# Keys of a large attention turned from their natural layout, two batches ahead, with the queries made in the other batch of each pair

## The chip, the cores and the metric

One NeuronCore of a Trainium2 chip runs the whole program. The metric is the device time of one execution in microseconds (us). The five engines of the core each work through their own list of instructions in order and wait for one another by semaphores: TensorE (PE, matrix products), VectorE (DVE), ScalarE (ACT), GpSimd (POOL) and SyncE (SP, which issues the DMA transfers).

## The reference

A small "perceiver": x is 32 batches of 64 rows of 256; a context is 32 batches of 1601 rows of 64. Two layers follow one another: attention to the context, self-attention and an MLP in the first; attention to the whole context, self-attention and a mixture of 16 experts in the second. The change touches only the second layer's attention to the context:

```python
q_hk = (hidden_q @ Wq.T).reshape(Bv, Sv, H, K)          # 64 rows, 16 heads of 128
q_big = apply_rope(einsum('bshk,hkq->bshq', q_hk, w_kc_q), sin_q, cos_q)
kv_r = apply_rope(kv_c, sin_k, cos_k)                   # 1601 keys of 64
q_r = einsum('bshq,hqr->bhsr', q_big, W_qr)
k_r = einsum('bld,hdr->bhlr', kv_r, W_kr)
attn = softmax(einsum('bhsr,bhlr->bhsl', q_r, k_r), axis=-1)
ctx_c = einsum('bhsl,bld->bhsd', attn, kv_r)            # then w_kc_kv and Wo
```

`apply_rope(x)` is `x * cos + rotate_half(x) * sin`, and rotate_half moves the upper half of the row in front with a changed sign. hidden_q is the layer-normalised x.

## The kernel before, in words

The matrices are combined once, so that a query of 64 numbers meets the rotated keys directly. The attention (`context_attention`) then runs over B = 32 batches of the context. Two batches share one block of 128 rows of x, so t counts NT = 16 pairs; e is 0 in the even batch 2t and 1 in the odd batch 2t+1. In each batch the 16 heads times 64 rows make 1024 columns of queries (two halves p of 512), and the 1601 keys are cut into NKT = 13 key tiles kt of 128 (the last has 65). In the text a "step" is one kt of `batch`. `batches` writes out batch 0 and the last three, and repeats a loop body of one odd and one even batch 14 times.

What one step of batch n does, by engine:

- PE: `scores` of the next key tile for p = 0 and 1 (two products into one bank, with k1 and k2), and `values` of this one. Each `scores` waits until ACT has taken the exponentials of the tile before it from the same bank. Between them, by third of a step, stand the pieces of other work: `max_scores` (16 pieces, scores of the next batch for its maxima, two banks mx in turn), `queries` (ten in five steps: `big`, then two later `effective`), `turn_keys`, `denominators` (step 0), `out` (OUT_AT = 4, even batch), `max_rows` (ROWS_AT = 10 and 11).
- ACT: `exps` of both halves, and the copies out of PSUM.
- DVE: `add` (the sum of the exponentials for p = 1), `reduce_max` (one for each of the 16 pieces; two banks, so a piece waits for the reduction two before it), `negate_max`, `invert` and `scale_heads` (steps 2 and 3), `rotate` and `split` (queries), `sum_keys` and `keep_kl` (keys), `normalise` and `update_x`.
- POOL: `add` for p = 0 and the two products of the keys' rotation.
- SP: `fetch` of the next context, twice (as it is and with its halves changed over).

Keys come from memory transposed (64 x 1608). They are rotated in four chunks of 402 columns (POOL lines 627 and 628, DVE line 977). ACT writes the rounded keys to k1 and to k2 (line 863), DVE the remainder to the lower half of k1 (line 982): k1 holds [kh; kl], k2 holds kh and a row of ones that adds minus the maximum. Thus the scores are exact to more than the rounded format. PE turns the sum kr in two parts at steps 6 and 7 to get the natural layout for `values` (kv). `max_scores` of the next batch reads k1 of the next batch, which is why k1 and k2 are kept at steps 0 and 1 of the batch before. The queries of pair t+1 are made in the odd batch, steps 0 to 4 (lines 703, 717 on PE, 1004 on DVE, 890, 891 on ACT), and its pieces for the maximum start at step 5; in the even batch they start at step 3. They end before ROWS_AT in both. x is normalised at step 10 of the even batch, and `turn_x` stands ahead of step 0 of the odd one. prob has three buffers in a ring and one for the last tile.

Of the kernel before, what the change touches and what calls it, by code (L numbers as in the profile page):

```python
# [481 lines left out]
def context_attention(nc, sb, pb, sem, a, x_all, const, wbig, mw, wvo):  # L482
# [12 lines left out]
    kcos = sb("cx_kcos", [DCX, SKP])  # L495
    ksin = sb("cx_ksin", [DCX, SKP])
    ctx = sb("cx_ctx", [DCX, SKP])
    ctxr = sb("cx_ctxr", [DCX, SKP])
    kr = sb("cx_kr", [DCX, SKP])
# [107 lines left out]
    with nc.Block() as block:  # L607

        @block.sync
        def _(sp):  # L610
            def fetch(n):
                sp.dma_start(ctx[:, :], a["cx_ctxT"][bass.ds(n, 1), :, :]).then_inc(s_ctx, 16)
                sp.dma_start(ctxr[:, :], a["cx_ctxrT"][bass.ds(n, 1), :, :]).then_inc(s_ctx, 16)

            fetch(0)
            with sp.Fori(1, B) as n:

                sp.wait_ge(s_kr, n * NKC)
                fetch(n)

        @block.gpsimd
        def _(pool):
            def rotate(n, c):
                cols = slice(c * KC, (c + 1) * KC)
                if c == 0:
                    pool.wait_ge(s_ctx, 32 * n + 32)
                pool.tensor_tensor(ctx[:, cols], ctx[:, cols], kcos[:, cols], ALU.mult)  # L627
                pool.tensor_tensor(ctxr[:, cols], ctxr[:, cols], ksin[:, cols], ALU.mult).then_inc(s_rope, 1)
# [1239 lines left out]
```

## Time and profile before

| | |
|---|---|
| time, median of 3 runs | 3492.59 us (3492.21 to 3497.96) |
| profiled execution: its time / its span | 3504.15 us / 3501.6 us |
| PE busy | 2942.5 us, 84% |
| DVE busy | 2084.2 us, 60% |
| ACT busy | 1277.2 us, 36% |
| POOL busy | 900.8 us, 26% |
| batch 6 (even), end to end | 1121.24 to 1170.48 us |
| batch 7 (odd), end to end | 1170.48 to 1240.73 us |

The span is what lies between the first and the last instruction of the profiled execution; the execution's own time is 2.6 us above it. Busy shares are means over stages with different limits. The attention that changes takes the stretch from about 690 to 2640 us. A batch ends where ACT copies the finished values out (line 928).

### The profile page before, as it was taken

How to read it: one execution, taken by the hardware profiler on the slowest of the kernel's cores; microseconds unless marked ns; L12 is line 12 of the kernel's file. 1: busy time of each engine (PE TensorE's matmuls, PEld its weight loads, DVE VectorE, ACT ScalarE, POOL GpSimd, SP SyncE). 2: the span in 40 equal slices, each digit the busy share in tenths (PEclk: the TensorE clock that was granted, in tenths of full speed). 3: DMA queues.
4: the chain of work that ended last, by engine and by line, in shares of the span. 5: the costliest groups of instructions: out<-in, count | busy, mean ns of one | idle time of the engine just before them, and what ended most of it. 6: DMA issues, size and time to landing. Idle time of an engine off the chain costs nothing. (4 is left out here: it accounts for less than half of the span.)

```text
span 3501.6 us, 51568 instructions
## 1 busy us (share of the span) xinstructions
PE 2942.5 (84%) x17592; PEld 1773.8 (51%) x17592; DVE 2084.2 (60%) x3249; ACT 1277.2 (36%) x2482; POOL 900.8 (26%) x784
## 2 busy tenths in 40 slices
PE   6767734579988988898898889888996889999999
PEld 3544412445544544454455445444543457777776
DVE  3445567357686777677776877686775643333332
ACT  3433312123344343434334433444343333333332
POOL 0001000134354444344434544453440000000000
PEclk9888856679999999999999999999999899999999
DMA  1000030000000000000000000000003000000000
GB/s 39 0 17 0 0 117 0 22 19 10 19 9 19 9 19 9 19 9 19 9 11 17 19 9 9 19 9 19 10 0 145 0 0 0 0 0 0 0 0 25
DMA packets 15045, 57.83 MB, mean 17 GB/s; under 512 B 2512, under 2 KB 7248, under 8 KB 13584
## 3 DMA queue, kind: packets, MB, share of 16 engines
q1 hardware_dynamic: 13392, 53.57, 5.5%
q10 hardware_dynamic: 1600, 3.56, 0.3%
q8 instruction: 32, 0.52, 0.1%
q14 instruction: 21, 0.17, 0.0%
HBM read 55.03 MB, written 2.10 MB: 16 GB/s over the span
## 5 line engine op out<-in xcount | busy, mean ns | idle before, releaser
L917 ACT ACTIVATE cx_prob<-cx_st 128x512 f32<-128x512 f32 (+1 forms) x832 | 477.4, 596 | 742.8 <-PE cx_st L774 680.7
L645 POOL TENSOR_TENSOR cx_acc<-cx_acc,cx_prob 128x512 f32<-128x512 f32 (+1 forms) x352 | 493.8, 1403 | 751.5 <-ACT cx_prob L917 747.4
L1023 DVE TENSOR_REDUCE cx_mhalf<-cx_mx 128x1 f32<-128x804 f32 x512 | 491.2, 983 | 86.5 <-PE cx_mx L747 83.7
L785 PE MATMUL cx_av<-cx_prob,cx_kv 128*64 128x512 f32 (+1 forms) x1664 | 462.2, 635 | 0.0
L773 PE MATMUL cx_st<-cx_q,cx_k 128*128 128x512 f32 (+1 forms) x832 | 372.5, 448 | 84.5 <-ACT cx_prob L917 60.5
L1506 PE MATMUL moe_gu<-moe_wgu,moe_xnT 128*128 128x352 f32 x1280 | 399.0, 463 | 0.0
L1044 DVE TENSOR_TENSOR cx_acc<-cx_acc,cx_prob 128x512 f32<-128x512 f32 (+1 forms) x352 | 371.3, 1055 | 21.7 <-ACT cx_prob L917 19.9
L747 PE MATMUL cx_mx<-cx_k,cx_q 128*128 128x402 f32 x1024 | 309.3, 388 | 53.2 <-DVE cx_mhalf L1023 47.3
L1641 DVE SCALAR_TENSOR_TENSOR moe_hid<-moe_silu,moe_coef,moe_gu 128x176 f32<-128x176 f32 x320 | 127.1, 397 | 351.6 <-ACT moe_silu L1569 349.4
L774 PE MATMUL cx_st<-cx_q,cx_k 128*128 128x512 f32 (+1 forms) x832 | 332.8, 400 | 0.0
L747 PEld LDWEIGHTS cx_mx<-cx_k,cx_q 128*128 128x128 f32 x1024 | 173.4, 195 | 264.0 <-DVE cx_mhalf L1023 216.8
L1506 PEld LDWEIGHTS moe_gu<-moe_wgu,moe_xnT 128*128 128x128 f32 x1280 | 242.2, 191 | 124.9 <-issue 7.5
L773 PEld LDWEIGHTS cx_st<-cx_q,cx_k 128*128 128x128 f32 (+1 forms) x832 | 154.5, 186 | 267.2 <-ACT cx_prob L917 157.9
L1004 DVE TENSOR_TENSOR cx_turn<-cx_mx,cx_tab 128x384 f32<-128x384 f32 x256 | 130.9, 553 | 264.5 <-PE cx_mx L703 264.5
L1569 ACT ACTIVATE moe_silu<-moe_gu 128x176 f32<-128x176 f32 x320 | 101.8, 318 | 372.0 <-PE moe_gu L1506 372.0
L1529 PE MATMUL moe_acc<-moe_wd,moe_hidT 128*128 128x256 f32 (+1 forms) x896 | 216.1, 382 | 0.0
L703 PE MATMUL cx_mx<-cx_xnT,cx_wbig 128*128 128x128 f32 x1536 | 205.6, 284 | 2.3 <-ACT cx_xnT L879 0.5
L703 PEld LDWEIGHTS cx_mx<-cx_xnT,cx_wbig 128*128 128x128 f32 x1536 | 184.2, 193 | 26.9 <-issue 16.4
L717 PE MATMUL cx_mx<-cx_turn,cx_mw 128*64 128x128 f32 (+1 forms) x2048 | 197.0, 296 | 0.0
L1529 PEld LDWEIGHTS moe_acc<-moe_wd,moe_hidT 128*128 128x128 f32 (+1 forms) x896 | 160.2, 190 | 21.9 <-issue 5.3
L1471 POOL TENSOR_TENSOR moe_rstd<-moe_mv,minus_half 128x1 f32<-128x1 f32 x16 | 8.8, 549 | 614.8 <-DVE moe_mv L1606 614.8
L627 POOL TENSOR_TENSOR cx_ctx<-cx_ctx,cx_kcos 64x402 f32<-64x402 f32 x128 | 160.5, 1254 | 7.3 <-DMA cx_ctxr<-in_cx_ctxrT 7.3
(214 smaller groups left out, 3945.0 us busy)
## 6 DMA issues: line engine op xcount, KB each, us to landing
cx_ctx<-in_cx_ctxT SPq DMA_DIRECT2D x32, 402.0 KB, 4.3
cx_ctxr<-in_cx_ctxrT SPq DMA_DIRECT2D x32, 402.0 KB, 5.5
moe_wgu<-in_moe_wgu SPq DMA_DIRECT2D x5, 1408.0 KB, 15.3
moe_wd<-in_moe_wd SPq DMA_DIRECT2D x4, 896.0 KB, 25.0
x_all<-in_x SPq DMA_DIRECT2D x1, 2048.0 KB, 5.3
cx_wq<-in_cx_wq SPq DMA_DIRECT2D x1, 2048.0 KB, 12.0
cx_woT<-in_cx_woT SPq DMA_DIRECT2D x1, 2048.0 KB, 29.5
out_x<-x_all SPq DMA_DIRECT2D x1, 2048.0 KB, 7.5
```

Source lines behind the costliest of these rows:

```text
L645: pool.tensor_tensor(acc[0][rows, :], sofar, prob[slot(kt)][rows, 0, :], ALU.add)\
L703: last = pe.matmul(mx[j % 2][:, 0, tile * P:(tile + 1) * P], wbig[:, c, j, tile * P:(tile + 1) * P], xnT[:, c, :], start=(c == 0), stop=(c ...
L717: last = pe.matmul(mx[j // 4][DCX * e:DCX * e + DCX, 1, at:at + P], mw[rows, j, cs, tile, :], turn[j % 2][rows, cs, tile, :, :], start=(cs ...
L747: last = pe.matmul(mx[b][:, h, 0:KQ], q, k1[e][:, lo:lo + KQ], start=True, stop=True)
L773: pe.matmul(st[p][0:nk(kt), :], k1[e][:, keys], q1[e][:, p, :, :], start=True, stop=False)
L774: pe.matmul(st[p][0:nk(kt), :], k2[e][:, keys], q2[e][:, p, :, :], start=False, stop=True)\
L785: last = pe.matmul(av[DCX * p:DCX * p + DCX, :], kv[e][0:nk(kt), kt, :], prob[slot(kt)][0:nk(kt), p, :], start=(kt == 0), stop=(kt == NKT ...
L917: act.activation(prob[slot(kt)][rows, p, :], st[p][rows, :], ACT.Exp).then_inc(s_exp, 1)
L1023: dve.tensor_reduce(mhalf[:, i // 2, i % 2:i % 2 + 1], mx[i % 2][:, :, 0:KQ], AX.XY, ALU.max)\
L1044: dve.tensor_tensor(acc[1][rows, :], sofar, prob[slot(kt)][rows, 1, :], ALU.add)\
L1506: last = pe.matmul(gu[i][:, 0:2 * FE], xnT[g][:, c, :], wgu[:, e, c, :], start=(c == 0), stop=(c == DC - 1))
L1529: last = pe.matmul(acc[:, 0:D], hidT[q % 2][0:n, k % 4, :], wd[0:n, k, :], start=(k == 0), stop=(k == NFC - 1))
```

## The change

All of it is in the attention to the whole context and in how its inputs are laid out.

- The context, its turned copy and the cos and sin tables are laid out in the natural way, as tiles of 128 keys: [128, 13, 64]. The rotation of a whole batch of keys is two POOL products (step 3) and one DVE addition (step 4) of 128 x 832 elements.
- ACT copies the rounded keys to khl[:, :, 0, :] (step 4) and DVE subtracts them into khl[:, :, 1, :] (step 5). PE transposes 13 tiles of 128 x 128 in four rounds at steps 6 to 9, ACT copies each round from PSUM to a new buffer kp (steps 7 to 10). kp holds what k1 held. `max_scores` reads kp.
- All that is done for batch n + 2 in batch n. SP issues two transfers from kp to k1 and to the upper half of k2 when the batch that used k1 and k2 is over; `scores` reads k1 and k2 as before, and now waits for the transfers.
- kv is a plain ACT copy of kr (step 2). The four copies that filled k1, k2 and kv from kr and PSUM in each batch are gone.
- The queries of pair t+1 are made in the even batch, steps 7 to 11; x is normalised there at step 5 and turned at the end of step 6. ACT's `keep_queries` and DVE's `split` stand at steps 0 and 1, and 1 and 2, of the odd batch. The even batch's 16 pieces lie in steps 1 to 6, the odd batch's in steps 3 to 9.

```diff
+    SUM_AT = 4
+    NORM_AT = 5
     TURN_AT = 6
+    QUERIES_AT = 7
     ROWS_AT = NKT - 3
-    SUM_AT = (8, 9, 11, 12)
     def pieces(e, kt, third):
-        start, end = 3 * (5 if e else 3), 3 * ROWS_AT
+        start, end = (9, 3 * ROWS_AT) if e else (4, 3 * QUERIES_AT)
...
+            def move(n, e):
+                sp.wait_ge(s_kp, KROUNDS * (n + 1))
+                if not isinstance(n, int) or n >= 2:
+                    sp.wait_ge(s_st, (n - 1) * 2 * NKT)
+                sp.dma_start(k1[e][:, :].bitcast(F32), kp[e][:, 0:SKP].bitcast(F32)).then_inc(s_kd[e], 16)
+                sp.dma_start(k2[e][0:DCX, :].bitcast(F32), kp[e][0:DCX, 0:SKP].bitcast(F32)).then_inc(s_kd[e], 16)
...
+            def rotate(n):                                                      # POOL, step 3
+                pool.wait_ge(s_ctx, 32 * n + 32)
+                pool.tensor_tensor(ctx[:, :, :], ctx[:, :, :], kcos[:, :, :], ALU.mult)
+                pool.tensor_tensor(ctxr[:, :, :], ctxr[:, :, :], ksin[:, :, :], ALU.mult).then_inc(s_rope, 1)
...
+            def turn_keys(n, r):
+                if r == 0:
+                    pe.wait_ge(s_kl, n + 1)
+                else:
+                    pe.wait_ge(s_kp, KROUNDS * n + r)
+                for kt in range(4 * r, min(4 * r + 4, NKT)):
+                    last = pe.transpose(misc[:, kt % 4 * P:(kt % 4 + 1) * P], khl[:, kt, :, :], ident[:, :])
                 last.then_inc(s_kt, 1)
...
-                    last = pe.matmul(mx[b][:, h, 0:KQ], q, k1[e][:, lo:lo + KQ], start=True, stop=True)
+                    last = pe.matmul(mx[b][:, h, 0:KQ], q, kp[e][:, lo:lo + KQ], start=True, stop=True)
...
             def batch(n, t, e, more, next):                                     # PE
                 for kt in range(NKT):
-                    if kt == 0 and more and e == 1:
-                        turn_x(t + 1)
                     for third in range(3):
...
-                        if more and e == 1 and third < 2 and kt <= CP // 2:
-                            queries(t + 1, 2 * kt + third)
+                        if more and e == 0 and third < 2 and 0 <= kt - QUERIES_AT <= CP // 2:
+                            queries(t + 1, 2 * (kt - QUERIES_AT) + third)
                         if next:
                             for i in pieces(e, kt, third):
                                 max_scores(t + e, n + 1, 1 - e, i)
+                    if kt == QUERIES_AT - 1 and more and e == 0:
+                        turn_x(t + 1)
...
-                    if kt in (TURN_AT, TURN_AT + 1) and next:
+                    if 0 <= kt - TURN_AT < KROUNDS and more:
...
-                        turn_keys(n + 1, kt - TURN_AT)
+                        turn_keys(n + 2, kt - TURN_AT)
...
             def batch(n, t, e, more, next):                                     # ACT
-                    if kt == 0 and more and e == 1:
-                        keep_x(t + 1)
                     if kt == 0 and e == 0:
                         odd_queries(t)
-                    if kt == 0 and next:
-                        keep_keys(n + 1, 1 - e, k1, s_k1)
-                    if kt == 1 and next:
-                        keep_keys(n + 1, 1 - e, k2, s_k2)
-                    if kt in (3, 4) and more and e == 1:
-                        keep_queries(t + 1, kt - 3)
-                    if kt in (TURN_AT + 1, TURN_AT + 2) and next:
-                        keep_kv(n + 1, 1 - e, kt - TURN_AT - 1)
+                    if kt in (0, 1) and more and e == 1:
+                        keep_queries(t + 1, kt)
+                    if kt == 2 and next:
+                        keep_kv(n + 1, 1 - e)
+                    if kt == SUM_AT and more:
+                        keep_kh(n + 2)
+                    if kt == QUERIES_AT and more and e == 0:
+                        keep_x(t + 1)
+                    if 0 <= kt - TURN_AT - 1 < KROUNDS and more:
+                        keep_turned(n + 2, t + 1, e, kt - TURN_AT - 1)
...
             def batch(n, t, e, more, next):                                     # DVE
-                        if third < 2 and more and e == 1 and kt < CP // 2:
-                            rotate(t + 1, 2 * kt + third)
+                        if third < 2 and more and e == 0 and 0 <= kt - QUERIES_AT < CP // 2:
+                            rotate(t + 1, 2 * (kt - QUERIES_AT) + third)
...
-                    if kt == 1 and next:
-                        keep_kl(n + 1, 1 - e)
+                    if kt in (1, 2) and more and e == 1:
+                        split(t + 1, kt - 1)
...
-                    if kt in (3, 4) and more and e == 1:
-                        split(t + 1, kt - 3)
+                    if kt == SUM_AT and more:
+                        sum_keys(n + 2)
+                    if kt == SUM_AT + 1 and more:
+                        keep_kl(n + 2)
...
-                    if more and kt in SUM_AT:
-                        sum_keys(n + 2, SUM_AT.index(kt))
-                    if more and e == 0 and kt == ROWS_AT:
-                        normalise(t + 1, base + (2 if next else 0))
+                    if kt == NORM_AT and more and e == 0:
+                        normalise(t + 1, base)
```

## Rows read from the trace of the kernel before

**Rows 1.** The page: the chain that ended last, share of the span by engine.

```profile
PE 18%; issue 0%; DVE 0%; POOL 0%; ACT 0%; POOLq 0%
```

**Rows 2.** Windows, batches 6 and 7: length, busy of PE, PEld, DVE, ACT, POOL, clock, DMA.

```profile
1121.24:1170.48 49.24, 42.10 (x188) 21.88 (x189) 40.79 (x46) 22.31 (x36) 27.40 (x21) 1.00 0.04 8
1170.48:1240.73 70.25, 64.03 (x398) 36.20 (x399) 46.31 (x60) 25.35 (x47) 24.61 (x20) 0.98 0.06 13
```

**Rows 3.** PE's timeline, batch 31, the last: two steps without other work (start, us, instruction).

```profile
2606.03 0.50 PE L773 MATMUL cx_st<-cx_q,cx_k 128*128 128x512 f32 x1
...
2608.16 0.50 PE L773 MATMUL cx_st<-cx_q,cx_k 128*128 128x512 f32 x1
```

**Rows 4.** PE's timeline in even batch 6: its waits, in brackets with their releaser.

```profile
1125.93 0.50 PE L773 MATMUL cx_st<-cx_q,cx_k 128*128 128x512 f32 x1 [1.76 <-ACT cx_prob L917]
...
1140.08 3.72 PE L802 MATMUL cx_misc<-cx_wvo,cx_heads 128*128 128x256 f32 x16 [1.43 <-DVE cx_heads L1055]
...
1164.28 0.22 PE L760 MATMUL cx_misc<-cx_identb,cx_nmh 128*1 128x128 bf16 x1 [1.35 <-DVE cx_nml L1031]
...
1168.25 0.47 PE L773 MATMUL cx_st<-cx_q,cx_k 128*128 128x512 f32 x1 [0.76 <-ACT cx_q L921]
```

**Rows 5.** PE's timeline in odd batch 5, from turn_x to the first piece.

```profile
1050.28 0.44 PE L693 MATMUL cx_mx<-ident,cx_xn 128*128 128x128 f32 x2
...
1055.56 1.03 PE L795 MATMUL cx_misc<-cx_acc,cx_ones 128*64 128x512 f32 x4
...
1085.17 1.08 PE L785 MATMUL cx_av<-cx_prob,cx_kv 128*64 128x512 f32 x4
1088.23 0.50 PE L773 MATMUL cx_st<-cx_q,cx_k 128*128 128x512 f32 x1 [1.98 <-ACT cx_prob L917]
```

**Rows 6.** Groups of instructions by line and shape, both batches: count, busy, mean ns, idle before.

```profile
L1023 DVE TENSOR_REDUCE cx_mhalf<-cx_mx 128x1 f32<-128x804 f32 x32 | 30.7, 982 | 5.5 <-PE cx_mx L747 5.3
...
L747 PE MATMUL cx_mx<-cx_k,cx_q 128*128 128x402 f32 x64 | 19.0, 381 | 3.2 <-DVE cx_mhalf L1023 3.0
...
L627 POOL TENSOR_TENSOR cx_ctx<-cx_ctx,cx_kcos 64x402 f32<-64x402 f32 x8 | 10.1, 1262 | 0.0
...
L1050 DVE RECIPROCAL cx_rden<-cx_misc 128x256 f32<-128x256 f32 x4 | 7.0, 1746 | 0.0
...
L863 ACT CAST cx_k<-cx_kr 64x1608 fp32r<-64x1608 f32 x4 | 6.1, 1529 | 0.0
...
L982 DVE TENSOR_TENSOR cx_k<-cx_kr,cx_k 64x1608 fp32r<-64x1608 f32 x2 | 3.7, 1827 | 0.1
...
L890 ACT CAST cx_q<-cx_mx 64x256 fp32r<-64x256 f32 x8 | 2.9, 368 | 8.8 <-PE cx_mx L717 8.7
```

**Rows 7.** DVE's timeline in even batch 6: the odd queries, out's shadow, the normalisation.

```profile
1123.85 1.22 DVE L1018 TENSOR_TENSOR cx_q<-cx_qs,cx_q 64x1024 fp32r<-64x1024 f32 x1 [5.63 <-ACT cx_q L899]
...
1144.66 1.00 DVE L1023 TENSOR_REDUCE cx_mhalf<-cx_mx 128x1 f32<-128x804 f32 x1 [2.23 <-PE cx_mx L747]
...
1164.77 0.42 DVE L988 BATCH_NORM_STATS2 cx_stats<-x_all 128x6 f32 x1
...
1166.26 1.34 DVE L996 TENSOR_SCALAR cx_xn<-x_all,cx_mv,cx_rstd 128x256 f32 x1 [0.66 <-POOL cx_rstd L632]
```

**Rows 8.** Lines 1044 (add) and 977 (sum_keys), 1000 to 2600 us: min/median/max ns.

```profile
L1044 DVE TENSOR_TENSOR cx_acc<-cx_acc,cx_prob x297: 671/823/1873, 1009.6 to 2597.2; 128x512 f32<-128x512 f32 x135, 65x512 f32<-65x512 f32 x14
...
L977 DVE TENSOR_TENSOR cx_kr<-cx_ctx,cx_ctxr x104: 555/561/1855, 1038.9 to 2551.8; 64x402 f32<-64x402 f32 x104
```

**Rows 9.** Windows of 1 us in odd batch 7, PE: busy, then clock, DMA.

```profile
1209.00:1210.00 1.00, 1.00 (x7) 0.94 0.00 0
...
1211.00:1212.00 1.00, 1.00 (x4) 0.50 0.00 0
...
1213.00:1214.00 1.00, 1.00 (x5) 0.86 0.00 0
```

**Rows 10.** The page's DMA issues: count, KB each, median us to landing.

```profile
cx_ctxr<-in_cx_ctxrT SPq DMA_DIRECT2D x32, 402.0 KB, 5.5
```

More of the change, by code:

```diff
@@ L494, in context_attention @@
     tab = sb("cx_tab", [P, 2, 3, S])
[L495 to L499, printed above, removed]
+    kcos = sb("cx_kcos", [P, NKT, DCX])
+    ksin = sb("cx_ksin", [P, NKT, DCX])
+    ctx = sb("cx_ctx", [P, NKT, DCX])
+    ctxr = sb("cx_ctxr", [P, NKT, DCX])
+    kr = sb("cx_kr", [P, NKT, DCX])
+    khl = sb("cx_khl", [P, NKT, 2, DCX])
+    kp = [sb(f"cx_kp{i}", [P, SKT], F32R) for i in range(2)]
     k1 = [sb(f"cx_k1{i}", [P, SKP], F32R) for i in range(2)]
@@ L611, in fetch, with before, batch @@
             def fetch(n):
[L612 to L619, printed above, removed]
+                sp.dma_start(ctx[:, :, :], a["cx_ctxN"][bass.ds(n, 1), :, :, :]).then_inc(s_ctx, 16)
+                sp.dma_start(ctxr[:, :, :], a["cx_ctxrN"][bass.ds(n, 1), :, :, :]).then_inc(s_ctx, 16)
+            def move(n, e):
[4 more added lines that the diff above has]
+                sp.dma_start(k2[e][0:DCX, :].bitcast(F32), kp[e][0:DCX, 0:SKP].bitcast(F32)).then_inc(s_kd[e], 16)
+            def before():
+                fetch(0)
+                sp.wait_ge(s_kr, 1)
+                fetch(1)
+                sp.wait_ge(s_set, 6)
+                move(0, 0)
+            def batch(n, t, e, more, next):
+                if more:
+                    sp.wait_ge(s_kr, n + 2)
+                    fetch(n + 2)
+                if next:
+                    move(n + 1, 1 - e)
+            batches(sp, before, batch)
         @block.gpsimd
         def _(pool):
[L623 to L628, printed above, removed]
+            def rotate(n):
+                pool.wait_ge(s_ctx, 32 * n + 32)
+                pool.tensor_tensor(ctx[:, :, :], ctx[:, :, :], kcos[:, :, :], ALU.mult)
+                pool.tensor_tensor(ctxr[:, :, :], ctxr[:, :, :], ksin[:, :, :], ALU.mult).then_inc(s_rope, 1)
             def root(t):
@@ L656, in before @@
                 root(0)
-                for n in range(2):
-                    for c in range(NKC):
-                        rotate(n, c)
+                rotate(0)
+                rotate(1)
             def batch(n, t, e, more, next):
@@ L808, in before @@
                 pe.wait_ge(s_one, 1)
-                turn_keys(0, 0)
-                turn_keys(0, 1)
+                for r in range(KROUNDS):
+                    turn_keys(0, r)
                 turn_x(0)
@@ L815, in before @@
                     max_scores(0, 0, 0, i)
-                max_rows(0, 0)
-                max_rows(0, 1)
-                scores(0, 0, 0, 0)
-                scores(0, 0, 0, 1)
+                for r in range(KROUNDS):
+                    turn_keys(1, r)
+                max_rows(0, 0, True)
+                max_rows(0, 1, True)
+                scores(0, 0, 0, 0, 0)
+                scores(0, 0, 0, 0, 1)
             def batch(n, t, e, more, next):
                 for kt in range(NKT):
-                    if kt == 0 and more and e == 1:
-                        turn_x(t + 1)
                     for third in range(3):
@@ L931, in before @@
                 act.wait_ge(s_set, 6)
-                keep_keys(0, 0, k1, s_k1)
-                keep_keys(0, 0, k2, s_k2)
-                keep_kv(0, 0, 0)
-                keep_kv(0, 0, 1)
+                keep_kh(0)
+                keep_kv(0, 0)
+                for r in range(KROUNDS):
+                    keep_turned(0, 0, 0, r)
                 keep_x(0)
@@ L938, in before @@
                     keep_queries(0, g)
+                keep_kh(1)
+                for r in range(KROUNDS):
+                    keep_turned(1, 0, 1, r)
                 keep_rows(0, 0, 0)
@@ L1066, in before @@
                 normalise(0, 0)
-                for c in range(NKC):
-                    sum_keys(0, c)
-                keep_kl(0, 0)
+                sum_keys(0)
+                keep_kl(0)
                 for j in range(CP):
@@ L1074, in before @@
                 split(0, 1)
-                for c in range(NKC):
-                    sum_keys(1, c)
+                sum_keys(1)
+                keep_kl(1)
                 for i in range(PIECES):
```

115 lines of the change are left out of this document (53 added, 62 removed).

## The prediction

> **What bounds the kernel now.** I read the chain that ended last first. Its row gives PE 18% and nobody else anything [rows 1], since that chain lies in the last stage and never reaches the attention; it says nothing about the change. So I went to the windows, one for each batch of a pair. An even batch takes 49.2 us, of which PE is busy 42.1 and DVE 40.8; an odd one takes 70.3, PE 64.0, DVE 46.3 [rows 2]. A pair is 119.5 us. No engine bounds it throughout: PE does in the steps that hold queries, DVE in the steps that hold three or more of the 16 maximum pieces. The timeline of PE shows the waits in between. A step with nothing else in it takes 2.13 us [rows 3], so 26 of them are 55.4 us of the pair, and the rest is the other work. The waits of the even batch are 1.76 us behind ACT's list of copies at step 0, 1.43 before `out`, 1.35 for `negate_max` and 0.76 for the row of the maximum [rows 4]. The odd batch has 1.98 us behind `keep_queries` at steps 3 and 4 [rows 5].
>
> What decides is how well DVE's work and PE's lie beside each other. DVE pays 0.98 us for one reduction (about 0.95 where they follow closely), PE at most 0.76 for the piece that it reduces (two matmuls of 0.38, which overlap; I take 0.45) [rows 6]. A step with three pieces costs DVE 2.85 plus an addition, PE 2.13 + 1.35 = 3.5.
>
> **The change, part by part.** *Copies of the keys.* Two ACT copies of 1.53 us leave steps 0 and 1 of each batch, and DVE's `keep_kl` of 1.83 us leaves step 1 [rows 6]. In the even batch the first stood between ACT's `odd_queries` and the next exponential, so the 1.76 us wait falls to about 0.3: gain 1.4. In the odd batch steps 0 to 4 are PE's, and nothing waited: 0. There `keep_queries` comes in, six copies of 0.37 for each half = 2.2 us a step at steps 0 and 1 [rows 6], between exponentials that PE needs after 2.13 us: a loss of 1.4. The 1.98 us wait at the end of the old query part goes with it.
>
> *Keys in 128 partitions.* The same POOL, DVE and ACT instructions on 832 elements instead of 1608. A POOL product of 402 takes 1.26 us [rows 6], so two of 832 take at most 5.2 us, against 8 x 1.26 = 10 before; POOL is busy for half of a batch [rows 2], and its part is hidden as long as the product pair of step 3 ends before DVE's step 4 does. DVE's sum: 402 take 0.56 at the median and 1.86 at worst [rows 8]; 832 take 1.1 to 2.4, I take 1.4, nearest to the median; before, four of 402 were 2.2 and more, spread over steps 8 to 12. `keep_kl` 1608 -> 832 gives 0.95 to 1.8, I take 1.05 (the row has the same width per element). `keep_kh` and `keep_kv` are 0.8 to 0.9 us of ACT each, in steps where ACT has two exponentials of 2.13 us free room: 0, and up to 0.9 a batch if ACT is late. Four copies of a round in steps 7 to 10: the same.
>
> *Turning keys.* 13 transposes of 128 x 128. Two of them took 0.44 us together with the pipe's fill [rows 5]; 0.1 to 0.22 each, I take 1.3 us a batch, as much as the two parts before. Nothing.
>
> *Transfers.* SP's list is fetch, then move, in each batch, and PE's first score of the next batch waits for the move. 402 KB land in 5.5 us [rows 10]. The two transfers are 1.2 MB, three times that; an estimate of 5.5 to 16.5 us, and they start when a batch starts, with over 40 us before they are needed. Price 0; late only beyond 40 us. `fetch` waits for the sum of step 4 of the batch before: over 25 us early.
>
> *Queries and pieces: the large part.* All ten query blocks go to steps 7 to 11 of the even batch, whose 16 pieces are pressed into steps 1 to 6, and `turn_x` stands behind the last of them. It waits for all 16 reductions and for `normalise`. I add up DVE's own list for the even batch from its first score on. `odd_queries` ends at 3.95 us as now (1123.85 + 1.22 - 1121.12) [rows 7]. Then until the last reduction: add(1) 1.4; five more additions of 0.92, between the median 0.82 and twice that [rows 8] = 4.6; 16 reductions of 0.95 = 15.2; two reciprocals 3.5 [rows 6]; `scale_heads` 1.0 (as an addition); the sum 1.4; `keep_kl` 1.05; `update_x` 0.4 (half an addition); `normalise` from 1164.77 to 1167.60 = 2.8, with POOL's root in it [rows 7]; and 1.2 of the 2.23 us that DVE now stands idle while PE does `out` [rows 7], since the sum covers the rest. Together 32.55, so `turn_x` starts at 36.5. PE has in those steps 6 x 2.13 + 16 x 0.45 + 3.7 = 23.7 us of work; it idles for the rest, in one gap of 5 us at the end. Beyond that point PE alone counts: from `turn_x` to the end of the fifth query step is 1050.28 to 1086.2 = 35.9, less `denominators` 1.0 [rows 5] = 34.9; key rounds 1.3; `max_rows` 1.1 (1168.25 - 1164.28 less a step and the wait) [rows 4]; step 12 with its wait 2.9. That is 40.2 (34.9 + 1.3 + 1.1 + 2.9). A gap also costs clock: after the 1.98 us gap TensorE was granted 0.50 (1.2 GHz) for some 3.4 us in this batch before 2.4 GHz came back [rows 9], and here that falls on query work: 1.7. Even batch: 78.4 us.
>
> Odd batch: PE starts step 3 at 8.8 (6.4 + 0.95 + 1.4). DVE from exp(1) at 4.0: nine additions 9.0, `split` 1.7, reciprocals 3.5, scale 1.0, sum 1.4, `keep_kl` 1.05, 16 reductions 15.2, idle 1.0: 37.9. `negate_max` then lies inside PE's step 10, and its 1.35 us wait is gone. PE's steps 3 to 9 hold 14.9 + 7.2 + 1.3 = 23.4 and end about 1 us before DVE, at 36.8, then 8.2 for steps 10 to 12 with the row wait: 45.0, I take 44.7.
>
> Pair 123.1 against 119.5: 3.6 us slower, fourteen times = 50. Outside the loop one pair's queries move from batch 29 to batch 0, about +25 and -25 (34.9 less five steps of 2.13, and the clock); batch 30 loses its key work, -2; the prologue turns two batches of keys, +2. The sum on the profiled execution (3504.15, span 3501.6) is 3554; that execution lies 11.6 above the median of the runs, so the median should be 3492.6 + 50, **about 3542 us**.
>
> *A rule.* A DVE addition took 0.67 to 1.87 us [rows 8], the long ones beside POOL's operations. The Trainium skill, "SBUF — State Buffer", section "SBUF: two separate sides", says that the port pair which VectorE and GpSimd share is an exclusive lock held for a whole instruction. By it the new POOL products, twice as long, would block an unlucky addition for up to 2.6 us instead of 1.3; the trace agrees in that no addition is longer than its own 0.67 plus one POOL product of 1.26. By that rule the even batch could be 1 us longer; the range covers it.
>
> **Rivals.**
> - *Less contention, faster.* POOL's rotation halves, and additions on the DVE lists could fall to their lone 0.67. For: the median is 0.82, so many are already nearly alone [rows 8]. Then the even list loses 0.7 + 1.2 + 0.6 (scale, sum), with a shorter gap no clock loss, 1.7; the odd list 3.0. Pair 115.9, 3.6 below now: 3442. It decides as soon as the two lists give back more than 3.6 us together. Against: the additions follow the same exponential on both engines, and POOL still does its 12 a batch.
> - *The clock falls twice.* PE has gaps of 1.3 and 2.3 us ahead of `out`. If the clock falls there too, `out`, a step and the pieces run at 1.2 GHz while DVE waits: 3 us a pair more, 3584. Against: `out`'s 1.43 wait did not do it.
> - *A wash.* PE's waits now are 1.76 + 1.43 + 1.35 + 1.98, all removed, and my two lists are too long by 3%: 3492.
> - *Transfers late.* If 1.2 MB between on-chip buffers took over 40 us, each us more would be paid in each of 31 batches; at 45 us 3650. Nothing in the rows speaks for a rate that low.
>
> **How the numbers follow.** Forecast 0.57, with its own range 3510 to 3572 (fourteen additions at 0.8 to 1.05 us on the two lists and the clock from 1 to 2 us: some 2.3 us a pair either way). Faster 0.20, clock twice 0.10, wash 0.08, late transfers 0.02, and 0.03 for what I don't see. The range for 8 in 10 is 3465 to 3590. A difference of 0.2%, 7 us, is about what can be told from none. Faster than that: 0.21 (the faster case and a little of the wash), within it 0.09, slower 0.70.
>
> **What would show it.** Right: even batches of 76 to 80 us and odd ones of 43 to 46 between ACT's copies of the finished values; PE idle some 5 us before `turn_x`, with DVE busy without a hole through steps 2 to 6; a clock of 0.50 after it; no wait of PE's first score on a transfer. Wrong: `turn_x` starting before 34 us of an even batch (the DVE list is shorter than summed), query steps of other than 8.1 us, additions with a mean under 0.8 us, or a wait on the moved keys.

## The result and the profile after

The changed kernel took 3657.93 us (median of 4, 3653.33 to 3662.26) against 3495.28 us (median of 4 of the kernel before on the same chip, 3492.21 to 3508.72): a ratio of 1.0457, 95% interval 1.0424 to 1.0491, slower. The forecast was 3542, the range 3465 to 3590: the direction was right, the size (50 us) less than a third of the 163 that came, and the time lies outside the range. The profiled execution took 3653.33 us with a span of 3651.5; 3504.15 and 3501.6 before. The difference of the spans is 149.9 us.

The page's chain that ended last is the same, and says as little about the change [rows 1]:

```profile
PE 18%; issue 0%; DVE 0%; POOL 0%; ACT 0%; POOLq 0%
```

The windows of an even and the next odd batch, cut at ACT's copies of the finished values as in [rows 2] (length, busy of PE, PEld, DVE, ACT, POOL, clock, DMA share, GB/s):

```profile
1145.94:1224.71 78.77, 68.04 (x412) 41.31 (x413) 42.58 (x59) 22.75 (x38) 20.76 (x15) 0.96 0.09 28
1224.71:1275.63 50.92, 40.05 (x170) 20.23 (x171) 38.17 (x40) 24.02 (x47) 19.94 (x14) 0.93 0.12 39
```

The even batch is 78.8 us where 78.4 was forecast, the odd one 50.9 where 44.7 was. Over the loop the mean pair is 129.7 us, and 119.7 before: 10.0 more, fourteen times = 140. Outside the loop, between the starts of the same copies: the prologue and batch 0 took 35.2 more, batch 29 19.1 less, batch 30 2.0 less, together 14. That is the whole of the 154.2 us by which the attention stage grew. The stages ahead of it were 8.7 shorter and the one behind 4.3 longer. The change doesn't touch them: with the same code there, the attention's first matrix product began at 634.11 us in this run and at 648.07 in e1's below, so these differences come from run to run.

The forecast pair was 123.1, 6.6 us short of what came, and 6.2 of the 6.6 lie in the odd batch. PE's timeline there shows one gap that [rows 4, 5] have nothing like:

```profile
1228.13 0.51 PE L795 MATMUL cx_st<-cx_q,cx_k 128*128 128x512 f32 x1 [0.47 <-ACT cx_prob L945]
...
1231.37 0.50 PE L795 MATMUL cx_st<-cx_q,cx_k 128*128 128x512 f32 x1 [1.02 <-ACT cx_prob L945]
...
1239.86 0.64 PE L764 MATMUL cx_mx<-cx_kp,cx_q 128*128 128x402 f32 x2 [1.85 <-DVE cx_mhalf L1049]
1240.34 0.39 PE L795 MATMUL cx_st<-cx_q,cx_k 128*128 128x512 f32 x1
...
1247.98 0.80 PE L795 MATMUL cx_st<-cx_q,cx_k 128*128 128x512 f32 x1 [5.45 <-ACT cx_prob L945]
...
1252.85 0.50 PE L795 MATMUL cx_st<-cx_q,cx_k 128*128 128x512 f32 x1
...
1269.43 0.22 PE L781 MATMUL cx_misc<-cx_identb,cx_nmh 128*1 128x128 bf16 x1 [1.16 <-DVE cx_nml L1057]
```

PE waits 5.45 us for an exponential. ACT is idle meanwhile, as its own timeline shows. Its list holds `keep_kh` (L887, the copy of the rounded keys) ahead of the two exponentials of scores that PE had finished by 1241:

```profile
1235.58 0.60 ACT L945 ACTIVATE cx_prob<-cx_st 128x512 f32<-128x512 f32 x1 [0.53 <-PE cx_st L796]
1246.55 0.89 ACT L887 CAST cx_khl<-cx_kr 128x832 fp32r<-128x832 f32 x1 [10.37 <-DVE cx_kr L1005]
1247.34 1.08 ACT L945 ACTIVATE cx_prob<-cx_st 128x512 f32<-128x512 f32 x2
```

`keep_kh` waits for DVE's sum of the keys, and that stands in DVE's list behind reductions, an addition, a reciprocal and the scaling. When it is done, DVE has nothing to reduce for 3.48 us, because PE could not make the next piece:

```profile
1236.77 2.13 DVE L1070 TENSOR_TENSOR cx_acc<-cx_acc,cx_prob 128x512 f32<-128x512 f32 x1
1238.83 1.88 DVE L1049 TENSOR_REDUCE cx_mhalf<-cx_mx 128x1 f32<-128x804 f32 x2
1240.63 1.74 DVE L1076 RECIPROCAL cx_rden<-cx_misc 128x256 f32<-128x256 f32 x1
...
1245.42 1.02 DVE L1005 TENSOR_TENSOR cx_kr<-cx_ctx,cx_ctxr 128x832 f32<-128x832 f32 x1
1249.92 1.00 DVE L1049 TENSOR_REDUCE cx_mhalf<-cx_mx 128x1 f32<-128x804 f32 x1 [3.48 <-PE cx_mx L764]
```

The waits view over 1000 to 2700 us gives the same for 26 batches (us in total, times, longest):

```profile
ACT cx_khl L887 <- DVE cx_kr L1005: 282.7, 26, 11.4
```

In the even batch the same wait is there, 11.37 us of it, but much of it runs while PE does pieces and `out`, and 0.73 us is left of it on PE. `turn_x`, which waits for the end of DVE's list there, starts where it was put (1182.39 − 1145.83 = 36.56 us from the batch's first score; forecast 36.5, with a gap of 5):

```profile
1169.70 0.88 ACT L887 CAST cx_khl<-cx_kr 128x832 fp32r<-128x832 f32 x1 [11.37 <-DVE cx_kr L1005]
```
```profile
1171.13 0.51 PE L795 MATMUL cx_st<-cx_q,cx_k 128*128 128x512 f32 x1 [0.73 <-ACT cx_prob L945]
...
1182.39 0.69 PE L711 MATMUL cx_mx<-ident,cx_xn 128*128 128x128 f32 x2 [5.02 <-DVE cx_mhalf L1049]
```

Windows of 1 us on PE (busy, clock, DMA share, GB/s), answering to [rows 9]: the granted clock fell to 0.50 (1.2 GHz) within each of the two gaps. It was back at 1.00 (2.4 GHz) at about 1187.6 and 1252.4, 5.2 and 4.4 us after PE had begun to work again.

```profile
1186.00:1187.00 1.00, 1.00 (x7) 0.50 0.00 0
...
1187.00:1188.00 1.00, 1.00 (x6) 0.72 0.00 0
...
1250.00:1251.00 1.00, 1.00 (x4) 0.50 0.22 87
...
1252.00:1253.00 1.00, 1.00 (x5) 0.80 0.00 0
```

The odd batch's first step after the gap, nearly all of it at that clock, took from 1247.98 to 1252.85, 4.87 us; the next, with the same two pieces, ran from 1252.85 to 1255.71, 2.86. So the gap cost PE 5.45 and then 2.0 more.

Groups by shape in both batches, answering to [rows 6] (count, busy, mean ns, idle before), then [rows 8] (min/median/max ns) and [rows 10] from the page (KB, us to landing):

```profile
L1005 DVE TENSOR_TENSOR cx_kr<-cx_ctx,cx_ctxr 128x832 f32<-128x832 f32 x2 | 2.0, 1018 | 0.0
...
L1009 DVE TENSOR_TENSOR cx_khl<-cx_kr,cx_khl 128x832 f32<-128x832 f32 x2 | 2.0, 1012 | 0.0
...
L894 ACT COPY cx_kv<-cx_kr 128x832 f32<-128x832 f32 x2 | 1.8, 888 | 0.0
...
L887 ACT CAST cx_khl<-cx_kr 128x832 fp32r<-128x832 f32 x2 | 1.8, 884 | 21.7 <-DVE cx_kr L1005 21.7
```
```profile
L1070 DVE TENSOR_TENSOR cx_acc<-cx_acc,cx_prob x291: 674/692/2166, 1002.4 to 2698.1; 128x512 f32<-128x512 f32 x132, 65x512 f32<-65x512 f32 x14
```
```profile
cx_k<-cx_kp SPq DMA_DIRECT2D x32, 804.0 KB, 3.9
...
cx_k<-cx_kp SPq DMA_DIRECT2D x32, 402.0 KB, 5.2
```

`keep_kl`, `keep_kv` and `keep_kh` have the durations that were forecast (1.05 and 0.8 to 0.9); the sum took 1.02 where 1.4 was taken. What was not forecast is 21.7 us of idle ACT ahead of the two `keep_kh`.

### The profile page after: what moved, and what is told of

Read it like the earlier page. It is cut to its first block and busy times, and to the rows that moved or that the text cites. A ratio compares the mean times of both kernels' runs of the same rounds, so it can differ in the third digit from the quotient of the medians.

```text
span 3651.5 us, 51264 instructions
## 1 busy us (share of the span) xinstructions
PE 2970.7 (81%) x17528; PEld 1824.3 (50%) x17528; DVE 1985.6 (54%) x3153; ACT 1261.3 (35%) x2514; POOL 721.3 (20%) x592
## 5 line engine op out<-in xcount | busy, mean ns | idle before, releaser
L668 POOL TENSOR_TENSOR cx_acc<-cx_acc,cx_prob 128x512 f32<-128x512 f32 (+1 forms) x352 | 467.1, 1327 | 1053.7 <-ACT cx_prob L945 1050.9
L795 PE MATMUL cx_st<-cx_q,cx_k 128*128 128x512 f32 (+1 forms) x832 | 383.4, 461 | 144.9 <-ACT cx_prob L945 122.4
L1070 DVE TENSOR_TENSOR cx_acc<-cx_acc,cx_prob 128x512 f32<-128x512 f32 (+1 forms) x352 | 361.4, 1027 | 96.0 <-ACT cx_prob L945 95.0
L764 PE MATMUL cx_mx<-cx_kp,cx_q 128*128 128x402 f32 x1024 | 316.3, 393 | 97.7 <-DVE cx_mhalf L1049 91.7
L796 PE MATMUL cx_st<-cx_q,cx_k 128*128 128x512 f32 (+1 forms) x832 | 340.4, 409 | 0.0
L764 PEld LDWEIGHTS cx_mx<-cx_kp,cx_q 128*128 128x128 f32 x1024 | 181.0, 201 | 299.2 <-DVE cx_mhalf L1049 239.7
L1030 DVE TENSOR_TENSOR cx_turn<-cx_mx,cx_tab 128x384 f32<-128x384 f32 x256 | 130.9, 553 | 355.6 <-PE cx_mx L721 355.6
L795 PEld LDWEIGHTS cx_st<-cx_q,cx_k 128*128 128x128 f32 (+1 forms) x832 | 164.1, 197 | 293.3 <-ACT cx_prob L945 232.8
L721 PE MATMUL cx_mx<-cx_xnT,cx_wbig 128*128 128x128 f32 x1536 | 223.0, 301 | 0.5 <-ACT cx_xnT L907 0.5
L721 PEld LDWEIGHTS cx_mx<-cx_xnT,cx_wbig 128*128 128x128 f32 x1536 | 205.2, 210 | 22.3 <-issue 16.5
L1557 PEld LDWEIGHTS moe_acc<-moe_wd,moe_hidT 128*128 128x128 f32 (+1 forms) x896 | 160.4, 190 | 21.7 <-issue 5.3
L796 PEld LDWEIGHTS cx_st<-cx_q,cx_k 128*128 128x128 f32 (+1 forms) x832 | 163.8, 197 | 6.6
L903 ACT CAST cx_kp<-cx_misc 128x512 fp32r<-128x512 f32 (+1 forms) x128 | 64.8, 506 | 271.0 <-PE cx_misc L702 271.0
```

What stands on the lines that cost most here:

```text
L668: pool.tensor_tensor(acc[0][rows, :], sofar, prob[slot(kt)][rows, 0, :], ALU.add)\
L721: last = pe.matmul(mx[j % 2][:, 0, tile * P:(tile + 1) * P], wbig[:, c, j, tile * P:(tile + 1) * P], xnT[:, c, :], start=(c == 0), stop=(c ...
L764: last = pe.matmul(mx[b][:, h, 0:KQ], q, kp[e][:, lo:lo + KQ], start=True, stop=True)
L795: pe.matmul(st[p][0:nk(kt), :], k1[e][:, keys], q1[e][:, p, :, :], start=True, stop=False)
L796: pe.matmul(st[p][0:nk(kt), :], k2[e][:, keys], q2[e][:, p, :, :], start=False, stop=True)\
L1070: dve.tensor_tensor(acc[1][rows, :], sofar, prob[slot(kt)][rows, 1, :], ALU.add)\
```

## The experiments

Main theory: the missing 6 us a pair are `keep_kh`, one step too early in ACT's list; the rest of the loss is the queries' move, in the even batch's DVE list. Rivals: the moved keys (e2 and e3 keep them), contention between POOL's longer products and DVE, and the clock alone; no run isolates the last two. Lengths are means over the loop's 14 pairs, in us; each ratio is to the kernel before on the same chip.

| kernel | median us | ratio, 95% | pair | odd | even |
|---|---|---|---|---|---|
| before | 3494 to 3505 | 1 | 119.7 | 70.4 | 49.3 |
| after | 3657.93 | 1.0457, 1.0424 to 1.0491 | 129.7 | 50.9 | 78.8 |
| e1, keep_kh late | 3557.60 | 1.0177, 1.0152 to 1.0202 | 123.7 | 46.4 | 77.2 |
| e2, queries back | 3457.50 | 0.9886, 0.9857 to 0.9915 | 116.7 | 71.3 | 45.4 |
| e3, both | 3396.49 | 0.9729, 0.9700 to 0.9759 | 113.2 | 68.4 | 44.8 |
| e4, old keys, queries moved | 3748.60 | 1.0736, 1.0704 to 1.0767 | 135.7 | 54.3 | 81.4 |
| d5, two more at step 5 | 3677.93 | 1.0483, 1.0455 to 1.0512 | 130.9 | 50.7 | 80.3 |
| d9, two more at step 9 | 3667.37 | 1.0445, 1.0406 to 1.0483 | 129.7 | 50.9 | 78.8 |
| h1, half reductions | 3433.17 | 0.9795, 0.9767 to 0.9823 | 116.0 | 42.2 | 73.8 |
| f3, e3 spread, sum early | 3380.92 | 0.9647, 0.9622 to 0.9672 | 111.9 | 67.4 | 44.4 |
| f2, e3 sum early | 3391.14 | 0.9701, 0.9663 to 0.9739 | 112.6 | 67.8 | 44.8 |
| g1, f2 heads early | 3430.13 | 0.9803, 0.9768 to 0.9838 | 114.9 | 68.0 | 46.9 |
| g2, g1 spread | 3409.24 | 0.9740, 0.9703 to 0.9776 | 113.5 | 67.1 | 46.4 |

**e1: keep_kh a step later.**

```diff
-                    if kt == SUM_AT and more:
+                    if kt == SUM_AT + 1 and more:
                         keep_kh(n + 2)
```

> The changed kernel with one line moved: ACT copies the rounded keys (keep_kh) after the exponentials of step 5 instead of step 4. Theory A (the odd batch's excess is ACT's in-order list: keep_kh at step 4 waits for DVE's sum_keys, which stands behind DVE's reductions, and the exponentials of step 5 wait behind it): PE's 5.45 us wait in the odd batch goes, the odd batch falls from 50.9 to 45 to 46.5 us, the even one by under 1, and 14 pairs and the edges give 65 to 95 us: 3565 to 3595. Rival B (the odd batch is bound by DVE's own list, ACT's wait only stands beside it): under 15 us. Rival C (the on-chip transfers or the new layout slow something down): no change at all.

The ratio fell from 1.0457 to 1.0177 by one line's place; the time of 3557.6 is 7 us below what theory A gave. The waits over the same stretch, then PE's two longest waits for an exponential in an odd batch and its wait for `negate_max`:

```profile
ACT cx_khl L887 <- DVE cx_kr L1005: 140.5, 26, 5.9
```
```profile
1096.46 0.50 PE L795 MATMUL cx_st<-cx_q,cx_k 128*128 128x512 f32 x1 [1.01 <-ACT cx_prob L945]
...
1113.09 0.50 PE L795 MATMUL cx_st<-cx_q,cx_k 128*128 128x512 f32 x1 [0.78 <-ACT cx_prob L945]
...
1130.06 0.22 PE L781 MATMUL cx_misc<-cx_identb,cx_nmh 128*1 128x128 bf16 x1 [1.15 <-DVE cx_nml L1057]
```

ACT still waits 140.5 us in all, but for PE the gap of 5.45 has become one of 0.78. The odd batch gained 4.5 and the even one 1.6, together 6.0 of the 6.6 us that the forecast pair was short. With the line here the kernel's pair is 123.7 where 123.1 was forecast. Not all of the gap's 5.45 + 2.0 us came back: without it PE waits oftener for DVE's reductions ahead of a piece (100 times and 93.3 us in the stretch, for 65 and 76.4).

Batch 0 lies outside the loop and had the same gap, with PE's longest wait for an exponential in it:

```profile
778.79 0.79 PE L795 MATMUL cx_st<-cx_q,cx_k 128*128 128x512 f32 x1 [3.45 <-ACT cx_prob L945]
```

In e1 it's gone, and the prologue with batch 0 takes 29.2 us more than before, where it was 35.2. Batch 29 fell from 50.5 to 46.2.

**e2: queries back, keep_kh still early. e3: both.** In both, `turn_x`, the query blocks, their rotations and their copies stand in the odd batch as before, and the pieces of the even batch are spread again; keys, buffers and transfers stay new.

```diff
-        start, end = (9, 3 * ROWS_AT) if e else (4, 3 * QUERIES_AT)
+        start, end = 3 * (5 if e else 3), 3 * ROWS_AT
...
-                        if more and e == 0 and third < 2 and 0 <= kt - QUERIES_AT <= CP // 2:
-                            queries(t + 1, 2 * (kt - QUERIES_AT) + third)
+                        if more and e == 1 and third < 2 and kt <= CP // 2:
+                            queries(t + 1, 2 * kt + third)
```

> The changed kernel with the queries (and x's normalisation, and the spread of the pieces) back where they were before: odd batch, steps 0 to 4. The keys' new path stays, keep_kh at step 4. Theory A and the list sum (the even batch of the change is DVE's list followed by PE's queries, 5 us of PE idle between them): the even batch keeps the blocked list, about 50 us, the odd one has its sum in the query steps where DVE is free, 67 to 69: pair 117 to 119, 3460 to 3500. Rival C (transfers and layout cost): stays above 3600.

> Queries back and keep_kh one step later, together. If the two causes are separate places, their gains add up except in the odd batch, whose block is already gone with the queries back: the even batch falls to 46 to 48 us, pair 114 to 116, 3420 to 3455, faster than the kernel before. If ACT's block was not a cause: the same as the run with the queries back alone.

Both are faster than the kernel before, e2 by 1.1% and e3 by 2.7%. So what the change does to the keys is a gain, 6.5 us a pair (119.7 to 113.2) with `keep_kh` in its late place, and what it does to the queries is the loss: 10.5 us a pair (113.2 to 123.7) with it late, 13.0 with it early. In e2 PE waits 4.78 us for an exponential in an odd batch, the block of `keep_kh` again; it costs 3.5 us a pair there (116.7 less 113.2) and 6.0 in the changed kernel.

The totals came out 3 and 24 us below what had been expected, and the split of e2 was wrong: its even batch took 45.4 us and not about 50, its odd one 71.3 and not 67 to 69. The block had not gone from the odd batch with the queries back; of e3's gain over e2 2.9 us a pair lie there and 0.6 in the even batch.

**e4: the kernel before with the queries moved, its keys as they were.**

```diff
-        start, end = 3 * (5 if e else 3), 3 * ROWS_AT
+        start, end = (9, 3 * ROWS_AT) if e else (6, 3 * QUERIES_AT)
...
+                    if kt == QUERIES_AT - 1 and more and e == 0:
+                        turn_x(t + 1)
```

> The kernel before with only the queries moved to steps 7 to 11 of the even batch, normalisation at step 5, and its pieces in steps 2 to 6 (they need k1, which is ready only at step 1). Keys as before. By the list sum: even batch 79 to 81 us (DVE's list to step 6 is 38, PE's part behind it 41), odd batch 46 to 49 (key copies and query copies now share ACT's steps 0 and 1): pair 126 to 129, 3580 to 3630. If it is the keys' path that costs, this one stays within 20 us of the kernel before.

A miss: 3748.6, well above what was expected. The even batch, 81.4 us, is near the expected 79 to 81; the odd one, 54.3, is 5 us over its 46 to 49. The queries' move alone costs 16.0 us a pair with the old keys. ACT's timeline in an odd batch shows part of why: the old keys' casts and `keep_queries` now share steps 0 and 1.

```profile
1106.01 1.09 ACT L919 ACTIVATE cx_prob<-cx_st 128x512 f32<-128x512 f32 x2
1106.98 1.53 ACT L865 CAST cx_k<-cx_kr 64x1608 fp32r<-64x1608 f32 x1
...
1110.68 1.08 ACT L919 ACTIVATE cx_prob<-cx_st 128x512 f32<-128x512 f32 x2
```

From one pair of exponentials to the next is 4.67 us, where a step of PE's needs one in 2.13 [rows 3]. In this case the two parts of the change are not additive: the new keys are worth more with the queries in the even batch.

**d5 and d9: added work on DVE.** Two reductions of a resident tile (128 x 832 each) are added to DVE's list in each even batch, ahead of `turn_x` (step 5) or behind it (step 9).

```diff
+                    if kt == 5 and e == 0:
+                        for i in range(2):
+                            dve.tensor_reduce(extra[:, i:i + 1], kcos[:, :, :], AX.XY, ALU.max)
```

> The changed kernel with two more DVE reductions (of a constant table, 832 elements, about 1 us each, result unused) in each even batch at step 5. If DVE's list up to the last piece sets when turn_x starts, they are paid in full: even batch 78.8 -> 80.8 us, PE's wait before turn_x 5.0 -> 7.0, 16 even batches give 28 to 34 us more than the changed kernel: 3685 to 3693. If PE or ACT sets the even batch: no change.

> The same two reductions at step 9 of each even batch, among the query blocks. If only PE counts behind turn_x: the even batch stays at 78.8 us and the time within 5 us of the changed kernel's 3658. If DVE's total work in the batch counts: as at step 5, 28 to 34 us more.

At step 5, PE's wait ahead of `turn_x` grew by 1.84 us and the even batch by 1.5, where 2.0 was expected; at step 9, neither moved. The totals differ too little to tell the two apart (their intervals overlap, and d5's overlaps the changed kernel's), the batch lengths do: 79.5 to 81.5 against 78.8. DVE's list up to `turn_x` sets the start of the queries, and 2 us more behind it cost nothing.

```profile
1195.18 0.69 PE L712 MATMUL cx_mx<-ident,cx_xn 128*128 128x128 f32 x2 [6.86 <-DVE cx_mhalf L1050]
```

**h1: e1 with half of each reduction.** Half of the keys are left out of the maximum.

```diff
-                dve.tensor_reduce(mhalf[:, i // 2, i % 2:i % 2 + 1], mx[i % 2][:, :, 0:KQ], AX.XY, ALU.max)
+                dve.tensor_reduce(mhalf[:, i // 2, i % 2:i % 2 + 1], mx[i % 2][:, 0:1, 0:KQ], AX.XY, ALU.max)
```

> The changed kernel with keep_kh one step later, and every maximum piece reduced over one bank of 402 columns instead of both (half of the keys are left out of the maximum). Each reduction falls from 0.98 to about 0.56 us, DVE's list in each batch by 6.7. If the lists bound both batches: the 5 us wait before turn_x vanishes, even batch 77 to 78 -> 71 to 72, odd batch 46.4 -> 42.5 to 44 (PE's own work is the floor there), 3558 -> 3415 to 3450. If the queries' position costs because of PE itself: less than 30 us.

A reduction fell from 0.98 to 0.56 us, sixteen of them 6.7 us, and the even batch by 3.4 (77.2 to 73.8): half of it came back, and less than had been expected (71 to 72). The odd batch fell by 4.2, to 42.2. The time is within the expected span all the same. The gap ahead of `turn_x`, which should have vanished, is still 4.24 us, with a short tail of DVE behind the last pieces:

```profile
1127.52 1.02 DVE L1009 TENSOR_TENSOR cx_khl<-cx_kr,cx_khl 128x832 f32<-128x832 f32 x1
1128.45 0.42 DVE L1087 TENSOR_TENSOR x_all<-cx_misc,x_all 128x256 f32 x1
1128.79 0.42 DVE L1014 BATCH_NORM_STATS2 cx_stats<-x_all 128x6 f32 x1
...
1130.28 1.34 DVE L1022 TENSOR_SCALAR cx_xn<-x_all,cx_mv,cx_rstd 128x256 f32 x1 [0.67 <-POOL cx_rstd L655]
1131.54 0.56 DVE L1049 TENSOR_REDUCE cx_mhalf<-cx_mx 128x1 f32<-128x402 f32 x1
1132.02 1.33 DVE L1070 TENSOR_TENSOR cx_acc<-cx_acc,cx_prob 128x512 f32<-128x512 f32 x1
1133.28 0.56 DVE L1049 TENSOR_REDUCE cx_mhalf<-cx_mx 128x1 f32<-128x402 f32 x1
```

DVE stood idle 4.71 us before that (0.44, 0.26, 0.74, 2.52 and 0.75 in front of a piece), so in steps 1 to 5 DVE often waited for PE. Lighter reductions alone do not close the gap: `keep_kl`, `update_x`, the normalisation and two pieces stand in one chain behind PE's last step of work, 1127.52 to 1133.84 = 6.3 us.

**f3, f2: a better place for the sum.** On e3, the odd batch's products, sum and copies two steps earlier (f2), and with it the even batch's pieces from the second third of step 1, the odd ones' as before (f3).

```diff
-    SUM_AT = 4
+    SUM = (4, 2)
...
-        start, end = 3 * (5 if e else 3), 3 * ROWS_AT
+        start, end = (15 if e else 4), 3 * ROWS_AT
```

> Queries back, keep_kh late, and two more moves that the traces point to: the even batch's pieces spread over steps 1 to 9 (kp is ready a batch ahead), and in the odd batch the keys' rotation, sum and remainder at steps 1 to 3, where DVE stands idle beside PE's queries. The even batch holds waits of 0.4, 1.4 (heads) and 0.5 us: 44.8 -> 43.5 to 44.5. The odd batch loses 1.0 + 1.7 us of DVE's list in steps 5 to 9: 68.7 -> 66 to 67.5. Pair 113.5 -> 110 to 111.5, 3396 -> 3345 to 3370. Rival: the pieces at steps 1 and 2 of the even batch push DVE's reciprocals back, out waits longer, and the even batch gains nothing or loses up to 1 us.

> The kernel with the queries back in the odd batch and keep_kh at step 5, and in the odd batches the products, the sum of the keys and its two copies two steps earlier (steps 1, 2, 3, 3 in place of 3, 4, 5, 5); the even batch's pieces stay as they were before. If of the two moves of the last version the sum was the one that helped (odd batches 68.4 to 67.4, since the sum then no longer stands among the reductions), pairs come to 111.9 to 112.5, a time of 3375 to 3385. If the spread of the even pieces did it, pairs stay at 113.2, 3396.

f3 is the best kernel here: 0.9647 (0.9622 to 0.9672) of the kernel before. It's 11 us slower than had been expected, and f2 lies between its two cases. The sum gives 0.5 us a pair (e3 to f2, 113.16 to 112.63), the spread 0.8 more (f2 to f3, 111.87). By the totals the intervals of e3 and f2 overlap and those of f2 and f3 touch, so that each helps rests on the batch lengths of one trace each. Its even batches were either 44.1 or 45.8 us; in one of the long ones `out` took 5.41 us at the lower clock in place of 3.72.

**g1 and g2: heads a step earlier.** PE waits 1.36 us for the heads ahead of `out` in f2.

```diff
-    HEADS_AT = 2
+    HEADS_AT = 1
```

> As the kernel with the early sums, and the reciprocal and the scaling of the last batch's heads one step earlier (step 1 in place of 2). PE waits 1.36 us for the heads before out in each even batch. If the DVE list from step 0 is what sets the heads, that wait goes: even batches 44.8 to 43.5, time 3355 to 3370. If they only push back the piece reductions and exponentials' additions by as much, or PE's granted clock falls after another gap, no change or up to 1 us a batch slower: 3375 to 3395.

> The same with the even batch's 16 pieces starting a third of a step into step 2, ahead of the place where out stands. If the pieces ahead of step 5 take the place of a wait of PE's (as expected where DVE has 2 us idle beside out), 0 to 0.7 us a pair less than g1: 3340 to 3370. If they get in the way of the reciprocals, up to 1 us more: 3355 to 3385.

Both are misses, slower than either of their cases. g2, with the pieces begun earlier, gets back 1.4 us of g1's 2.3 a pair and is still behind f2. In g1 the wait moved instead of going. PE in an even batch of f2, and of g1 (ahead of its `out`, at 1109.17, there is none left):

```profile
1099.99 0.64 PE L764 MATMUL cx_mx<-cx_kp,cx_q 128*128 128x402 f32 x2 [0.38 <-DVE cx_mhalf L1049]
...
1104.03 3.72 PE L824 MATMUL cx_misc<-cx_wvo,cx_heads 128*128 128x256 f32 x16 [1.36 <-DVE cx_heads L1081]
...
1114.15 0.64 PE L764 MATMUL cx_mx<-cx_kp,cx_q 128*128 128x402 f32 x2 [0.52 <-DVE cx_mhalf L1049]
```
```profile
1102.88 0.64 PE L764 MATMUL cx_mx<-cx_kp,cx_q 128*128 128x402 f32 x2 [1.86 <-DVE cx_mhalf L1049]
...
1105.25 1.04 PE L764 MATMUL cx_mx<-cx_kp,cx_q 128*128 128x402 f32 x2 [1.26 <-DVE cx_mhalf L1049]
```

DVE does the two reciprocals (1.74 each) first, and the pieces wait for its reductions: 1.86 + 1.26 (+ 0.52 later) against 0.38 + 1.36 + 0.52, 1.4 us more. The two gaps stand close together, and the window 1102.80 to 1107.00 has a mean clock of 0.75, where f2's 1100 to 1108 had 1.00. The clock doesn't fall each time: nine of g1's 14 even batches took 47.4 to 47.5 us with a mean clock of 0.96, the other five 45.9 to 46.0 at 1.00, with waits of 1.85 and 1.27 in the one below (length, PE busy, clock, DMA share, GB/s). So the waits cost 1.2 us of f2's 44.8, and the clock 1.5 more where it falls; the mean batch is 2.1 longer.

```profile
976.75:1022.73 45.98, 41.20 (x186) 1.00 0.14 45
1090.56:1137.96 47.40, 42.70 (x186) 0.96 0.14 44
```

## Why the prediction missed

- **The even batch: right, with some luck in the sizes.** DVE's list to `turn_x` was put at 36.5 us and took 36.56; d5 and d9 show that it is this list that counts. That the sum came out to 0.1 us is luck, since single terms were off and cancelled: the first addition 1.77 for 1.4, the scaling 0.69 and the sum 1.02 for 1.0 and 1.4, DVE's idle time beside `out` 2.69 for 1.2. From `turn_x` to the end it was 42.2 for 41.9. The clock fell where it was said to, but PE worked at the lower one for 5.2 us and not 3.4, so that its share is nearer 2.6 us (half of 5.2, an estimate) than 1.7. The rest then took 39.6 where 40.2 had been summed.
- **The odd batch: the step that failed** is the one on the keys' copies: "in steps where ACT has two exponentials of 2.13 us free room: 0, and up to 0.9 a batch if ACT is late". It priced `keep_kh` by its length (0.89 us, right) and by ACT's room (ACT is busy 24 of 51 us, right), and left out what it waits for. It stands in step 4 of ACT's list, its input in step 4 of DVE's list, and that list runs late, with the reductions, the reciprocals and the scaling ahead; the exponentials queue behind. The prediction had the sum in DVE's list at its place, but did not ask which engine needs it first, or what stands behind that instruction. By e1 this is worth 6.0 us a pair, 84 us over the loop, and 10 more in batches 0 and 29: 94 of the 104 us by which the attention stage exceeded its forecast. With the line a step later the kernel took 3557.6, inside the range.
- **What is left in e1's odd batch**, 46.4 for 44.7. PE still waits 0.78 us behind `keep_kh`, the same mechanism as the big gap, and 1.15 for `negate_max`, a wait that the prediction said was gone; DVE's last reductions end too late for it. The waits behind `keep_queries`, 0.47 and 1.01, had been priced at 1.4. The sum itself gave 45.0, and no reason stands for taking 44.7.
- **The edges.** The prologue and batch 0 were put at +27 and took 35.2 more, batch 29 at −25 and gave 19.1: 14 in all where 0 was forecast. In e1 they are +29.2 and −23.3 (69.6 to 46.2), together 4 with batch 30: 10 of the 14 us are `keep_kh` again, and 2 us of the prologue and batch 0 stay unexplained.
- **The rivals.** *Less contention*: the median addition did fall from 823 to 692 ns [rows 8], but additions in the pair still have a mean of 1017 ns, and the longest rose from 1873 to 2166; one of 2.13 us stood beside a POOL product of 1.96. *The clock falls twice*: it did, but behind the odd batch's new gap and not ahead of the even batch's `out`; the gap is the cause, the clock adds 2.0 us to it. *Late transfers*: no; 804 KB landed in 3.9 us at the median, and no score waited on them. (The rival's 3650 was counted from the time before; from the forecast the same 5 us in 31 batches would give 3697.) *A wash*: no.
- **Not stated as a case, though the terms held it:** the keys alone are a gain. I had given them 1.4 us and less list; e3 shows 6.5 us a pair.

On the addition that took 2.13 us: it began at 1236.77, and POOL's product ran from 1236.40 to 1238.36, so that 0.54 us of the addition lie behind its end, most of the 0.67 that one takes alone. POOL's own next addition began at 1238.31, before DVE's was over at 1238.90, and took 1.71 us where 1.27 is usual. This is about what a lock between the two would give. The Trainium skill, "SBUF — State Buffer", section "SBUF: two separate sides", has VectorE and GpSimd share a port pair by an exclusive lock held for a whole instruction; the trace agrees, by these two rows and DVE's above.

```profile
1236.40 1.96 POOL L651 TENSOR_TENSOR cx_ctxr<-cx_ctxr,cx_ksin 128x832 f32<-128x832 f32 x1
1238.31 1.71 POOL L668 TENSOR_TENSOR cx_acc<-cx_acc,cx_prob 128x512 f32<-128x512 f32 x1
```

## What to carry to other kernels

An instruction that is added to an engine with plenty of idle time is free only if its input is ready when its turn comes: where the input comes from the engine with the longest list, write down the time at which that list gets there, and put the reader a step behind. Everything behind it in order waits too, and the waits view shows it in one line (282.7 us at L887).

Work that is moved from one half of a pair into the other is priced by the engine that is full where it arrives. Here the queries pressed DVE's 16 reductions into six steps, and PE stood 5 us. And a change of two parts should be run apart: the good one (the keys, 6.5 us a pair) was hidden by the bad one (the queries, 10.5) until then.

## What was not expected of the hardware

- An on-chip transfer of 804 KB landed in 3.9 us, and the 402 KB issued behind it in 5.2; from DRAM 416 KB took 3.2 to 4.0.
- After PE's gaps of 5.02 and 5.45 us the granted clock was 0.50 (1.2 GHz), and full again 5.2 and 4.4 us after work began. In batch 7 of the kernel before, after the 1.98 us gap of the row below, it fell only at about 1209.9, 1.6 us after PE had gone back to work, and was full again at about 1213.3, 5.0 us after [rows 9]. In g1 two waits of 1.86 and 1.26 us within 4.3 us brought it down in nine batches of 14 and left it at 1.00 in five.

```profile
1208.31 0.50 PE L773 MATMUL cx_st<-cx_q,cx_k 128*128 128x512 f32 x1 [1.98 <-ACT cx_prob L917]
```

- A reduction of half the columns took 0.56 us for 0.98. If the time grows evenly with the columns, 402 of them cost 0.42 and 0.14 is fixed, an estimate from these two sizes.
